# Adapter and MLP with a routed expert: two batches per step, the up projection by seven block products, split weights streamed from DRAM

## The chip, the cores and the metric

One core of one Trainium2 chip runs the whole kernel. The metric is the device time of one execution in microseconds (us), as a median of several executions; 3 runs of the kernel before are known.

## The reference

```python
x = x + L0(x, lang)     # x: 16 batches x 512 tokens x 512
x = x + L1(x, expert)

# L0: adapter with the weights of the batch's language (10 languages)
h = relu(x @ W1[lang] + b1[lang])              # 512 -> 128
u = x + h @ W2[lang] + b2[lang]                # 128 -> 512
L0 = (u - mean(u)) * rsqrt(var(u) + 1e-5) * gamma[lang] + beta[lang]

# L1: MLP; the last 128 output columns come from the batch's expert (8 experts)
h = gelu(x @ W1 + b1)                          # 512 -> 2048, shared weights
L1 = concat(h @ W2 + b2, h @ We[expert] + be[expert])   # 2048 -> 384 | 128
```

All of it is float32.

## The kernel before

Engines are written in raw form: each of PE, ACT, DVE (VectorE), POOL (GpSimd) and SP has its own program, ordered by hand, and waits on semaphores. SP issues all the DMAs. Batches are taken one at a time: the first is unrolled, 14 run in a hardware loop, the last is unrolled (`run`). While the MLP of batch i runs, the adapter of batch i+1 runs in between (`m` in the code).

A float32 operand is split in two rounded halves, hi and lo: ACT copies to a rounded tile (hi), DVE or POOL subtracts (lo), and PE adds three products (`three_passes`, L130 to L132). One such product has a 128x128 stationary and a 128x512 moving operand.

The MLP works on x1T, the transposed input of 4 chunks of 128 features by 512 tokens. For each of the 16 hidden chunks j (HC), `pe_up_step` makes 4 chunks x 3 passes = 12 matmuls into one of two PSUM banks; ACT applies the Gelu (L192) and rounds (L202), DVE makes the lo half (L240). `pe_down_step` for chunk j-2 (LAG) adds 4 token tiles x 3 passes = 12 matmuls to four PSUM banks that stay open over all 16 chunks. At the end DVE adds each bank to the residual tile (L290) and SP stores it.

The split MLP weights w1 and the shared 384 columns of w2 are made once, during the first batch (`load_weights`, `act_weights_hi`, `dve_weights_lo`), and stay in SBUF. The expert's 128 columns are loaded for each batch and split by POOL in 8 pairs of chunks (`pool_expert`, L337 and L339).

Adapter of the next batch: PE up (12 matmuls), PE down (12), 16 transposes of 128x128 (L184); DVE and POOL do the normalization (`dve_moments`, `dve_finish`, `pool_biases` L312 and L314, `pool_rsqrt` L318). POOL also makes the residual tiles (`pool_residual`, L324), which wait until the last store of that tile is done (`out_done`). The numbers XT, A1, RELU, A2 and LN give the hidden chunk beside which each step stands:

```python
XT, A1, RELU, A2, LN = 2, 3, 7, 8, 9
```

## Time and profile before

| | |
|---|---|
| runs, us | 1562.46, 1563.09, 1563.63 (median 1563.09) |
| profiled execution, span from first to last instruction | 1562.4 us |
| PE matmul | 1527.2 us busy (98%), 6784 matmuls |
| DVE | 598.0 us (38%), 948 instructions |
| ACT | 438.6 us (28%), 706 instructions |
| POOL | 620.2 us (40%), 580 instructions |
| DMA | 96.93 MB, mean 62 GB/s |

The profile has no other time for its own execution than the span; it lies 0.7 us under the median of the runs. Busy time counts an instruction from its start to its end. Matmuls overlap, so the step from one start to the next tells what one costs. PEclk in the windows is the granted TensorE clock: 1.00 is 2.4 GHz, 0.50 is 1.2 GHz.

### The profile page before, as it was taken

How to read it: one execution, taken by the hardware profiler on the slowest of the kernel's cores; microseconds unless marked ns; L12 is line 12 of the kernel's file. 1: busy time of each engine (PE TensorE's matmuls, PEld its weight loads, DVE VectorE, ACT ScalarE, POOL GpSimd, SP SyncE). 2: the span in 40 equal slices, each digit the busy share in tenths (PEclk: the TensorE clock that was granted, in tenths of full speed). 3: DMA queues.
4: the chain of work that ended last, by engine and by line, in shares of the span. 5: the costliest groups of instructions: out<-in, count | busy, mean ns of one | idle time of the engine just before them, and what ended most of it. 6: DMA issues, size and time to landing. Idle time of an engine off the chain costs nothing.

```text
span 1562.4 us, 20500 instructions
## 1 busy us (share of the span) xinstructions
PE 1527.2 (98%) x6784; PEld 1255.1 (80%) x6784; DVE 598.0 (38%) x948; ACT 438.6 (28%) x706; POOL 620.2 (40%) x580
## 2 busy tenths in 40 slices
PE   3899999999999999999999999999999999999999
PEld 2678888888888888888888888888888888888887
DVE  6664343432434333344333434334343333443311
ACT  1442222222232322323232222322323223232222
POOL 4464427243262523526244272432625235262300
PEclk7899999999999999999999999999999999999999
DMA  5523013040120402104030130401204021030100
GB/s 177 155 87 114 27 48 92 7 129 10 52 87 10 129 10 87 53 12 124 10 120 20 50 89 7 129 10 57 83 10 129 10 87 52 12 124 10 36 0 27
DMA packets 67121, 96.93 MB, mean 62 GB/s; under 512 B 9632, under 2 KB 30240, under 8 KB 67104
## 3 DMA queue, kind: packets, MB, share of 16 engines
q1 hardware_dynamic: 67104, 96.71, 20.4%
q8 instruction: 10, 0.16, 0.0%
q14 instruction: 7, 0.06, 0.0%
HBM read 79.90 MB, written 16.78 MB: 62 GB/s over the span
## 4 chain that ended last, share of the span: by engine, by line
PE 94%; DMA 2%; DVE 2%; SPq 1%; POOL 1%; issue 0%; ACT 0%; ACTq 0%; POOLq 0%
PE down L130 15%; PE down L132 15%; PE down L131 15%; PE up L132 14%; PE up L130 14%; PE up L131 14%; PE aux L184 2%; PE aux L132 2%; DMA resid<-m_w 2%; PE aux L131 2%; PE aux L130 2%; DVE w_lo L247 1%; DVE x L284 0%; DMA expert_raw<-m_we 0%; SPq L363 0%
## 5 line engine op out<-in xcount | busy, mean ns | idle before, releaser
L240 DVE TENSOR_TENSOR g_lo<-g_raw,g_hi 128x512 fp32r<-128x512 f32 x256 | 224.8, 878 | 696.1 <-ACT g_hi L202 696.0
L130 PE MATMUL down<-w_hi,g_hi 128*128 128x512 f32 x1024 | 407.2, 398 | 0.0
L132 PE MATMUL down<-w_hi,g_lo 128*128 128x512 f32 x1024 | 400.5, 391 | 0.0
L130 PE MATMUL up<-x1T_hi,w_hi 128*128 128x512 f32 x1024 | 399.4, 390 | 0.0
L132 PE MATMUL up<-x1T_hi,w_lo 128*128 128x512 f32 x1024 | 399.1, 390 | 0.0
L131 PE MATMUL up<-x1T_lo,w_hi 128*128 128x512 f32 x1024 | 399.1, 390 | 0.0
L131 PE MATMUL down<-w_lo,g_hi 128*128 128x512 f32 x1024 | 398.6, 389 | 0.0
L192 ACT ACTIVATE g_raw<-up,m_b_sb 128x512 f32<-128x512 f32 x256 | 176.3, 689 | 536.5 <-PE up L132 536.5
L202 ACT CAST g_hi<-g_raw 128x512 fp32r<-128x512 f32 x256 | 159.5, 623 | 485.8 <-PE down L132 483.7
L337 POOL TENSOR_TENSOR w_hi<-expert_raw,ones 128x256 fp32r<-128x256 f32 x128 | 80.7, 630 | 506.0 <-PE down L132 471.1
L132 PEld LDWEIGHTS down<-w_hi,g_lo 128*128 128x128 f32 x1024 | 192.1, 188 | 43.8
L131 PEld LDWEIGHTS down<-w_lo,g_hi 128*128 128x128 f32 x1024 | 192.7, 188 | 40.3
L131 PEld LDWEIGHTS up<-x1T_lo,w_hi 128*128 128x128 f32 x1024 | 192.8, 188 | 40.1
L130 PEld LDWEIGHTS up<-x1T_hi,w_hi 128*128 128x128 f32 x1024 | 192.8, 188 | 40.0
L132 PEld LDWEIGHTS up<-x1T_hi,w_lo 128*128 128x128 f32 x1024 | 192.6, 188 | 40.1
L130 PEld LDWEIGHTS down<-w_hi,g_hi 128*128 128x128 f32 x1024 | 192.3, 188 | 38.6
L318 POOL TENSOR_TENSOR rstd<-var_eps,minus_half 128x1 f32<-128x1 f32 x64 | 63.4, 990 | 317.3 <-DVE var_eps L276 317.3
L339 POOL TENSOR_TENSOR w_lo<-expert_raw,w_hi 128x256 fp32r<-128x256 f32 x128 | 130.9, 1023 | 10.1
L251 DVE TENSOR_TENSOR xT_lo<-xT_raw,xT_hi 128x512 fp32r<-128x512 f32 x64 | 61.2, 957 | 109.4 <-ACT xT_hi L221 109.4
L312 POOL TENSOR_TENSOR x<-x_sb,b_bc 128x512 f32<-128x512 f32 x64 | 94.5, 1476 | 17.3 <-DMA x_sb<-x 15.2
L324 POOL TENSOR_TENSOR resid<-x,m_bias 128x512 f32<-128x512 f32 x64 | 94.6, 1511 | 0.0
L314 POOL TENSOR_TENSOR x_sb<-x_sb,beta_bc 128x512 f32<-128x512 f32 x64 | 84.8, 1325 | 5.0
(44 smaller groups left out, 830.6 us busy)
## 6 DMA issues: line engine op xcount, KB each, us to landing
xT_raw<-xT SPq DMA_DIRECT2D x64, 256.0 KB, 4.1
x_sb<-x SPq DMA_DIRECT2D x64, 256.0 KB, 7.1
expert_raw<-m_we SPq DMA_DIRECT2D x128, 128.0 KB, 2.1
out<-resid SPq DMA_DIRECT2D x64, 256.0 KB, 2.2
a_w_raw<-a_w SPq DMA_DIRECT2D x32, 256.0 KB, 2.8
b_bc<-a_b SPq DMA_DIRECT2D x16, 256.0 KB, 3.7
beta_bc<-a_beta SPq DMA_DIRECT2D x16, 256.0 KB, 5.4
gamma_bc<-a_gamma SPq DMA_DIRECT2D x16, 256.0 KB, 6.8
```

The lines of the kernel that those rows point to most:

```text
L130: eng.matmul(bank, a_hi, b_hi, start=first, stop=False)
L131: eng.matmul(bank, a_hi, b_lo, start=False, stop=False)
L132: return eng.matmul(bank, a_lo, b_hi, start=False, stop=last)
L192: eng.activation(g_raw[:, j % 2, :], up[j % 2][:, :], ACT.Gelu, bias=m_b1_sb[:, j:j + 1]).then_inc(act_g, 1)
L202: eng.copy(g_hi[:, j % 2, :], g_raw[:, j % 2, :]).then_inc(act_ghi, 1)
L240: eng.tensor_tensor(g_lo[:, j % 2, :], g_raw[:, j % 2, :], raw(g_hi[:, j % 2, :]), ALU.subtract).then_inc(dve_glo, 1)
L312: eng.tensor_tensor(x1[:, t, :], x_sb[:, t, :], b2_bc[:, :], ALU.add).then_inc(pool_xb, 1)
L314: eng.tensor_tensor(x_sb[:, t, :], x_sb[:, t, :], beta_bc[:, :], ALU.add).then_inc(pool_xb, 1)
L318: eng.tensor_tensor(rstd[:, t:t + 1], var_eps[:, t:t + 1], minus_half[:, :], ALU.pow).then_inc(pool_rstd, 1)
L324: eng.tensor_tensor(resid[:, t, :], x1[:, t, :], m_bias[:, :], ALU.add).then_inc(pool_res, 1)
L337: eng.tensor_tensor(w2_hi[:, js, cols], expert_raw[:, p % 2, :, :], ones[:, :, :].to_broadcast([P, 2, PART]), ALU.mult).then_inc(pool_eh, 1)
L339: eng.tensor_tensor(w2_lo[:, js, cols], expert_raw[:, p % 2, :, :], raw(w2_hi[:, js, cols]), ALU.subtract).then_inc(pool_e, 1)
```

## The change

Batches are taken in pairs (8 of them: first, 6 in the loop, last), and hidden chunk k is taken with chunk k+8: 8 groups per pair. With A the weights (2 blocks of hidden by 2 blocks of input features) and B the transposed inputs (2 blocks of features by 2 batches), the four outputs C11, C12 (first and second batch, chunk k) and C21, C22 (chunk k+8) are formed from seven products P1 to P7 of sums of blocks. Each product is 2 chunks of 128 features x 3 passes = 6 matmuls.

- A has three given blocks in use as they are, and four sums S1 to S4. POOL makes the sums once, in the first pair, ACT and DVE split all seven (1792 columns a group), PE uses them from one of two slots, and SP writes the split group to DRAM (`keep_w1`, `keep_w2`). In later pairs SP loads group k+1 while k runs: 128x3584 words of w1 and 128x1536 of w2 for each group.
- B has three blocks and four sums T1 to T4, made for each pair from the transposes: DVE sums, ACT rounds, POOL (T) or DVE (B) makes the lo half.
- Three PSUM banks take the products. ACT copies P1 away (s1), DVE makes five sums a group (q, u2, c12, c22, c21), then ACT applies the Gelu.
- The down projection of both batches shares the four banks in turn. A batch keeps them for two groups, then DVE adds them to the residual (`dve_down_sum`).
- The input chunks, adapter and normalization of both batches of the next pair are spread over groups 0 to 7. Both batches of the first pair run their adapter ahead of the first product.

The order in the new kernel, cut to what the prediction speaks of:

```diff
+    def product(eng, bank, k, of_w, of_x, opens, closes):
+        for c in range(2):
+            s = slice(c * P, (c + 1) * P)
+            last = three_passes(eng, bank[:, :], w1[:, k % 2, HI, of_w, s], w1[:, k % 2, LO, of_w, s],
+                                bo[:, of_x, c, HI, :], bo[:, of_x, c, LO, :], opens and c == 0, closes and c == 1)
...
+    def pe_p7(eng, i, k):
+        eng.wait_ge(dve_u2, i.count(GROUPS, k + 1))
+        product(eng, up_b, k, S3, T3, False, False).then_inc(pe_p[7], 1)
...
+    def pe_down(eng, pr, b, k):
...
+        eng.wait_ge(pool_e[b], pr.count(GROUPS, k + 1))
...
     def pe_iteration(eng, i, m):
-        for j in range(HC):
-            pe_up_step(eng, i, j)
...
+        for k in range(GROUPS):
+            pe_p1(eng, i, k)
+            if m and k == 4:
+                pe_adapter_up(eng, m, 1, 0)
+            if m and k == 7:
+                eng.wait_ge(dve_x1, m.count(2 * TT, 2 * TT))
+                pe_transpose(eng, m, 1, 0)
+            pe_p5(eng, i, k)
...
+            if k % 2 == 0:
+                if k >= 2:
+                    pe_down(eng, i, 0, k - 1)
+                elif i is not first:
+                    pe_down(eng, prev, 0, GROUPS - 1)
+            else:
+                if k >= 2:
+                    pe_down(eng, i, 1, k - 2)
+                elif i is not first:
+                    pe_down(eng, prev, 1, GROUPS - 1)
+            if m and k == 1:
+                pe_adapter_up(eng, m, 0, 2)
...
+            pe_p6(eng, i, k)
...
+            pe_p2(eng, i, k)
+            pe_p3(eng, i, k)
...
+            pe_p7(eng, i, k)
...
+            if k % 2 == 0:
+                if k >= 2:
+                    pe_down(eng, i, 1, k - 2)
+                elif i is not first:
+                    pe_down(eng, prev, 1, GROUPS - 2)
+            else:
+                pe_down(eng, i, 0, k - 1)
...
+            pe_p4(eng, i, k)
+            if m and k == 7:
+                eng.wait_ge(dve_blo, m.count(6, 4))
+                eng.wait_ge(dve_t, m.count(8, 6))
+                pe_transpose(eng, m, 0, 2)
...
+    def pool_residual(eng, i, b, t):
...
+        if i is not first:
+            eng.wait_ge(out_done[b][t], i.count(16, 0))
+        eng.tensor_tensor(resid[:, b, t, :], x1[:, b, t, :], m_bias[:, b, :], ALU.add).then_inc(pool_res, 1)
...
+    def pool_iteration(eng, i, m):
...
+            if i is first and k < GROUPS - 1:
+                pool_weight_sums(eng, k + 1)
+            if k == 0:
+                if m:
+                    pool_aw(eng, m, 0, 0)
+                    pool_aw(eng, m, 0, 1)
+                for t in range(TT):
+                    pool_residual(eng, i, 0, t)
+            if k % 2 == 1:
+                pool_expert(eng, i, 0, k - 1)
+                pool_expert(eng, i, 1, k - 1)
+            if k == 1:
+                for t in range(TT):
+                    pool_residual(eng, i, 1, t)
+                if m:
+                    for t in range(TT):
+                        pool_biases(eng, m, 0, t)
...
+            if m and k == 3:
+                pool_aw(eng, m, 1, 0)
+                pool_aw(eng, m, 1, 1)
...
+            if k % 2 == 1:
+                pool_expert(eng, i, 0, k)
+                pool_expert(eng, i, 1, k)
...
     def sp_iteration(eng, i, m, first_expert=None):
...
+        if i is not first:
+            load_w1(eng, i, 1)
+            experts = expert_ids(eng, i)
+        language = languages(eng, m) if m else None
+        for k in range(GROUPS):
...
+            elif 1 <= k < GROUPS - 1:
+                load_w1(eng, i, k + 1)
...
+                if k == 1:
+                    load_xT(eng, m, 0, 2)
+                    load_xT(eng, m, 0, 3)
...
+            if i is not first and k < 2:
+                store(eng, prev, k)
...
+            else:
+                load_w2(eng, i, k)
+            if i is not first or k >= 2:
+                load_experts(eng, k, experts)
```

Two places of the new order. First POOL, in the loop: the residual tiles, the two bias sums of each token tile, and an expert's hi and lo halves. In the kernel before (L300, L302 split the adapter's weights) a batch's residual tiles and biases stand like this:

```order
L302 TENSOR_TENSOR aw_lo<-a_w_raw,aw_hi 128x512
L324 TENSOR_TENSOR resid<-x,m_bias 128x512 x4
L308 ISA
L312 TENSOR_TENSOR x<-x_sb,b_bc 128x512
L313 ISA
L314 TENSOR_TENSOR x_sb<-x_sb,beta_bc 128x512
L329 ISA
L334 ISA
L337 TENSOR_TENSOR w_hi<-expert_raw,ones 128x2x128
L339 TENSOR_TENSOR w_lo<-expert_raw,w_hi 128x2x128
L312 TENSOR_TENSOR x<-x_sb,b_bc 128x512
L313 REGISTER_ALU
```

In the changed kernel, group 1 of a pair in the loop (L781 residual of the second batch, L767 and L769 biases, L788 and L790 hi and lo of the expert for w2; the four bias pairs are alike, and two are left out here):

```order
L781 TENSOR_TENSOR resid<-x_68,m_bias 128x512 x4
L763 ISA
L766 REGISTER_ALU
L767 TENSOR_TENSOR x_68<-xs,vecs 128x512
L768 REGISTER_ALU
L769 TENSOR_TENSOR xs<-xs,vecs 128x512
...
L767 TENSOR_TENSOR x_68<-xs,vecs 128x512
L768 REGISTER_ALU
L769 TENSOR_TENSOR xs<-xs,vecs 128x512
L788 TENSOR_TENSOR w_51<-w_raw,ones 128x2x128
L789 REGISTER_ALU
L790 TENSOR_TENSOR w_51<-w_raw,w_51 128x2x128
```

The expert of group 1 now stands behind all four residual tiles and all eight bias sums; before, an expert stood behind the first two bias sums.

Second DVE, in the loop. In the kernel before, the lo half of an input chunk (L251) stands between two lo halves of the Gelu (L240):

```order
L240 TENSOR_TENSOR g_lo<-g_raw,g_hi 128x512
L250 ISA
L251 TENSOR_TENSOR xT_lo<-xT_raw,xT_hi 128x512
L239 REGISTER_ALU
L240 TENSOR_TENSOR g_lo<-g_raw,g_hi 128x512
```

In the changed kernel, group 1 (L539 is the sum q, L590 an input chunk's lo half, L584 the sum of a down bank, L545 the sum u2):

```order
L539 TENSOR_TENSOR q<-up_c,s_65 128x512
L589 REGISTER_ALU
L590 TENSOR_TENSOR xTs<-xTs_raw,xTs 128x512
L589 REGISTER_ALU
L590 TENSOR_TENSOR xTs<-xTs_raw,xTs 128x512
L583 REGISTER_ALU
L584 TENSOR_TENSOR resid<-down,resid 128x512
L583 REGISTER_ALU
L584 TENSOR_TENSOR resid<-down,resid 128x512
L583 REGISTER_ALU
L584 TENSOR_TENSOR resid<-down,resid 128x512 x2
L545 TENSOR_TENSOR u_66<-up_b,s_65 128x512
```

The down sums and u2 now stand behind the lo halves of two input chunks.

## Rows read from the trace of the kernel before

**Rows 1.** The page: span, busy time, and the chain that ended last
```profile
span 1562.4 us, 20500 instructions
PE 1527.2 (98%) x6784; PEld 1255.1 (80%) x6784; DVE 598.0 (38%) x948; ACT 438.6 (28%) x706; POOL 620.2 (40%) x580
PE 94%; DMA 2%; DVE 2%; SPq 1%; POOL 1%; issue 0%; ACT 0%; ACTq 0%; POOLq 0%
```

**Rows 2.** Window of one batch (length, busy by engine, PEclk, DMA share, GB/s)
```profile
224.48:319.25 94.77, 94.77 (x426) 78.17 (x425) 35.51 (x57) 26.26 (x42) 38.92 (x36) 1.00 0.19 59
```

**Rows 3.** Timeline of PE (start, us): first of 12 down, of 12 up, and next
```profile
201.79 0.40 PE L130 MATMUL down<-w_hi,g_hi 128*128 128x512 f32 x1
...
204.55 0.39 PE L130 MATMUL up<-x1T_hi,w_hi 128*128 128x512 f32 x1
...
207.27 0.39 PE L130 MATMUL aux<-aw_hi,h_hi 128*128 128x512 f32 x1
```

**Rows 4.** Windows of the start (columns as in rows 2)
```profile
10.00:20.00 10.00, 6.45 (x15) 4.19 (x16) 4.42 (x6) 3.11 (x6) 3.15 (x3) 0.87 0.96 304
20.00:30.00 10.00, 4.92 (x10) 2.38 (x9) 9.70 (x15) 1.49 (x4) 9.77 (x8) 0.50 0.77 251
16.00:18.00 2.00, 0.00 (x0) 0.00 (x0) 1.11 (x1) 0.82 (x2) 1.23 (x1) 0.85 1.06 408
```

**Rows 5.** Timeline of DVE: first and last of the four token tiles at the start
```profile
22.97 0.68 DVE L268 TENSOR_TENSOR x<-aux,x 128x512 f32<-128x512 f32 x1
...
35.52 1.76 DVE L284 SCALAR_TENSOR_TENSOR x<-x,rstd,x_sb 128x512 f32<-128x512 f32 x2
```

**Rows 6.** Timeline of PE: idle time and the matmuls around it at the start
```profile
15.09 0.40 PE L132 MATMUL aux<-xT_hi,aw_lo 128*128 128x512 f32 x1
18.73 0.77 PE L130 MATMUL aux<-aw_hi,h_hi 128*128 128x512 f32 x1 [3.25 <-DVE h_lo L256]
37.42 1.94 PE L184 MATMUL aux<-ident,x 128*128 128x128 f32 x8 [9.04 <-DVE x L284]
```

**Rows 7.** Groups of instructions (count, busy us, mean ns, idle before): POOL, DVE, ACT
```profile
L312 POOL TENSOR_TENSOR x<-x_sb,b_bc 128x512 f32<-128x512 f32 x64 | 94.5, 1476 | 17.3 <-DMA x_sb<-x 15.2 <-POOL resid L324 0.2
L314 POOL TENSOR_TENSOR x_sb<-x_sb,beta_bc 128x512 f32<-128x512 f32 x64 | 84.8, 1325 | 5.0
L337 POOL TENSOR_TENSOR w_hi<-expert_raw,ones 128x256 fp32r<-128x256 f32 x128 | 80.7, 630 | 506.0 <-PE down L132 471.1 <-DMA expert_raw<-m_we 34.9
L290 DVE TENSOR_TENSOR resid<-down,resid 128x512 f32<-128x512 f32 x64 | 39.8, 681 | 2.0 <-PE down L132 2.0
L260 DVE TENSOR_TENSOR x1T_lo<-aux,x1T_hi 128x512 fp32r<-128x512 f32 x64 | 42.6, 686 | 76.3 <-ACT x1T_hi L235 76.3
L202 ACT CAST g_hi<-g_raw 128x512 fp32r<-128x512 f32 x256 | 159.5, 623 | 485.8 <-PE down L132 483.7
```

**Rows 8.** Timeline of POOL in the loop: adapter weights' lo half, four residual tiles
```profile
147.87 1.29 POOL L302 TENSOR_TENSOR aw_lo<-a_w_raw,aw_hi 128x512 fp32r<-128x512 f32 x1
151.83 5.95 POOL L324 TENSOR_TENSOR resid<-x,m_bias 128x512 f32<-128x512 f32 x4
```

**Rows 9.** One tile's instructions (ns min/median/max): POOL's residual and expert lo half
```profile
L324 POOL TENSOR_TENSOR resid<-x,m_bias x64: 1287/1295/1747, 94.3 to 1477.3; 128x512 f32<-128x512 f32 x64
L339 POOL TENSOR_TENSOR w_lo<-expert_raw,w_hi x128: 725/1205/1212, 36.8 to 1472.9; 128x256 fp32r<-128x256 f32 x128
```

**Rows 10.** Timeline of SP around the reading of two ids
```profile
129.68 0.33 SPq L381 DMA_DIRECT2D m_bias<-m_be  x1
134.01 0.34 SPq L350 DMA_DIRECT2D a_w_raw<-a_w  x1
```

**Rows 11.** DMA issues (KB each, median us to landing), and landing of xT_raw's
```profile
out<-resid SPq DMA_DIRECT2D x64, 256.0 KB, 2.2
DMA to landing us min/median/max: 2.7/4.1/5.1
```

**Rows 12.** Window of PE's restart at the start (columns as in rows 2)
```profile
43.70:48.20 4.50, 4.50 (x13) 3.54 (x12) 2.83 (x5) 2.45 (x5) 0.00 (x0) 0.51 0.30 98
```

More of the change, by code:

```diff
@@ L75, in build, with sb @@
-    h0_raw = xT_raw[:, 0, :]
-    h0_hi, h0_lo = (sb(f"h0_{h}", [P, TOK], f32r) for h in ("hi", "lo"))
-    b2_bc, gamma_bc, beta_bc = (sb(n, [P, D]) for n in ("b2_bc", "gamma_bc", "beta_bc"))
-    a_b1_sb = sb("a_b1_sb", [P, 1])
+    GROUPS = HC // 2
+    WIDE = PART + SHARED + PART
+    A11, A12, S4, A22, S1, S2, S3 = range(7)
+    B11, B21, B22, T4, T1, T2, T3 = range(7)
+    C11, C12, C22, C21 = range(4)
+    place = [384]
+    def sb(name, shape, dt=f32, over=None):
+        size = 4
+        for n in shape[1:]:
+            size *= n
+        at = place[0] if over is None else homes[over]
+        if over is None:
+            place[0] += (size + 31) // 32 * 32
+        homes[name] = at
+        return nc.alloc_sbuf_tensor_at(name, shape, dt, offset=at)
@@ new lines, in act_xT_hi, with act_relu @@
+    def act_xT_hi(eng, m, b, k):
+        tile, values = xT_tile(m, b, k)
+        eng.wait_ge(in_xT[b][k], m.count(16, 16))
+        eng.copy(tile[:, HI, :], values[:, LO, :]).then_inc(act_xhi, 1)
+    def act_relu(eng, m, b, bank=aux):
+        tile, values = h0_tile(m, b)
+        eng.wait_ge(pe_a1, m.count(2 * KC, (b + 1) * KC))
+        eng.wait_ge(in_b1[b], m.count(16, 16))
+        if m is not first:
+            eng.wait_ge(pe_a2, m.count(2 * TT, b * TT))
+        eng.activation(values[:, LO, :], bank[:, :], ACT.Relu, bias=a_b1_sb[:, b:b + 1]).then_inc(act_h0, 1)
+        eng.wait_ge(act_h0, m.count(2, b + 1))
+        eng.copy(tile[:, HI, :], values[:, LO, :]).then_inc(act_h0hi, 1)
@@ new lines, in store, with languages @@
+    def store(eng, i, b):
+        for t in range(TT):
+            if b == 0:
+                eng.wait_ge(dve_out[0], i.count(4 * GROUPS, 3 * GROUPS + 2 * (t + 1)))
+            else:
+                eng.wait_ge(dve_out[1], i.count(2 * GROUPS, 3 * GROUPS // 2 + t + 1))
+            eng.dma_start(out[i.batch(b), t * P:(t + 1) * P, :], resid[:, b, t, :]).then_inc(out_done[b][t], 16)
+    def languages(eng, m):
+        return [eng.value_load(lang[0:1, bass.ds(m.batch(b), 1)], min_val=0, max_val=LANGS - 1) for b in range(2)]
@@ L591, in _ @@
[L591 to L601 removed]
+            dve_xT_lo(eng, first, 0, 0)
+            dve_xT_lo(eng, first, 0, 1)
@@ L602, in _ @@
+            dve_b_lo(eng, first, B11, 0, up_b)
+            dve_b_lo(eng, first, B11, 1, up_c)
+            dve_t1(eng, first, 0, up_b)
+            dve_t1(eng, first, 1, up_c)
+            dve_t3_t2(eng, first, 0, down[0])
+            dve_b_lo(eng, first, B22, 0, down[0])
+            dve_t3_t2(eng, first, 1, down[1])
+            dve_b_lo(eng, first, B22, 1, down[1])
             run(eng, dve_iteration)
+            dve_sum_c21(eng, last_pair, GROUPS - 1)
+            dve_g_lo(eng, last_pair, GROUPS - 1, C21)
```

1249 lines of the change are left out of this document (819 added, 430 removed).

## The prediction

> **What bounds the kernel now.** I read the page first: PE is 98% busy and 94% of the chain that ended last [rows 1]. Then the windows: one batch of the loop takes 94.77 us, all of them PE, with the clock at its upper level [rows 2]. 16 x 94.77 = 1516.3, so start and tail cost 1562.4 - 1516.3 = 46.1 us. Then PE's timeline for the price of one matmul: 12 down matmuls take 2.76 us, 0.230 each, and 12 up matmuls 2.72 us, 0.2267 each [rows 3]. So a matmul less is time less, as long as nothing else makes PE wait; and everything else stands beside PE with room in it (DVE 38%, POOL 40%). The question is where PE will wait.
>
> **PE's own work.** The seven products of a group are 7 x 6 = 42 matmuls, 336 in a pair instead of 384. 48 x 0.2267 = 10.9 us less in a pair. A pair's work is 189.5 - 10.9 = 178.7 us; eight pairs 1429.3. That is 87 us to win. Without waits a group takes: seven products of 1.36, two down blocks of 24 x 0.23 = 5.5, together 20.6 us; with two adapter pieces of 0.69, 21.9.
>
> **The start, up to the first held down block.** Both batches' adapters now stand ahead of the first product. DVE takes the second batch's second adapter weight ahead of the first token tile, and SP loads it last: behind it in the queue's order are 26 loads of 0.26 MB, 6.8 MB. The start moved 304 and 251 GB/s [rows 4], so 6.8 MB at 278 take 24.5 us, and with the first issues and the ids (some 7 us) it lands at 32. With ACT's and DVE's halves, 0.62 and 0.69 [rows 7], the first token tile starts at 33.5. Before, four tiles took from 22.97 to 35.52 + 1.76 = 37.28, 3.6 us a tile [rows 5]. Eight tiles 28.6, the split of the first 1792 weight columns 2.2 (686 ns for 512 [rows 7], less a fixed part), waits for POOL's reciprocal roots, which now queue behind its biases, 2.4, another half 0.7: 67.4. Then five sets of transposes at the lower clock, 1.94 / 2 = 0.97 each [rows 6], 72.3, P1 75; T1, T3, T2, T4 are made by DVE, ACT and POOL in turn, and POOL's eight lo halves at 1.29 [rows 8] to 1.48 [rows 7] let P6 go at about 81.5 and end at 82.8.
>
> From there POOL has one unbroken list before PE may take the down block of group 1 (it waits for that group's expert, which stands last, as the order shows): weight sums of 256 columns 4 x 0.8 = 3.2 (the size of the lo half [rows 9]), adapter weights 5.1 (lo, hi, lo took 3.96 [rows 8]), four residual tiles 5.95 [rows 8], sums 3.2, two experts 3.6, four residual tiles 5.95, four bias pairs 4 x (1.476 + 1.325 + 0.05) = 11.4, one expert 0.63 + 1.2 = 1.8 [rows 7, 9]: 40.2 us, so the block starts at 123.0. PE's work until then is 14.4 (both adapters, transposes), 11.3 (group 0), 16.4 (group 1) and 3.4: 45.6 at its prices. **Start: 77.4 us lost**, where the kernel before lost 46.1 - 3.4 = 42.7. Bounds: loads at 400 GB/s [rows 4] and POOL's shortest rows give 70; 85 with its longest.
>
> Later in the first pair the weight sums and splits delay POOL's and DVE's lists twice: DVE's 2.3 us ahead of the moments of group 3 and POOL's expert behind them 4.3, group 6 1.0: **5.3** (0 to 10).
>
> **The pairs of the loop.** I follow the waits of one pair; T0, T1 are the starts of its groups 0 and 1.
> - End of group 7: the last B22 chunk is transposed behind the down block; ACT 0.6, then DVE T3, T2 and lo half, 0.65 each [rows 7], before the shared bank is free for the next transpose. It ends 1.3 us after P4, and 0.2 are lost earlier: **1.5**, at 7 boundaries 10.5 (5 to 20).
> - Group 0: SP loads w1 (1.84 MB) when P4 ends (T0 - 1.8) and then reads four ids. Two took 4.0 us [rows 10], so four 8.0; xT is issued at T0 + 6.8 and lands 2.7 later [rows 11], ACT 0.65, twice, DVE's second half ends at T0 + 11.5. Only then DVE adds the down banks, eight pieces 2.9, and makes u2 at T0 + 15.0. P7 could start at T0 + 13.5: **1.5**.
> - Group 1: xT stands behind w2 and experts (issued 1.4 us before T1, 1.05 MB) and w1 (1.84 MB). At 400 GB/s [rows 4] xT lands at T1 + 9.3, its lo half is there at 10.65; the adapter matmul wants it at 8.2: **2.4**.
> - Group 2: DVE's second xT half ends at T1 + 11.4, the first down sum 0.6 later [rows 7], the store 0.4 + 2.2 [rows 11]: T1 + 14.6. POOL's residual tiles wait for it: 5.5 to 5.95, bias pairs 11.3, expert 1.5 to 1.8: 18.6, so T1 + 33.2. PE wants it at T1 + 21.9 + 2.4 + 3.4 = 27.8: **5.4**. Without the late xT it would be T1 + 9.4 + 18.6 = 28.0 against 25.4: 2.6 at least.
> - Group 4: POOL's root of group 3 ends at 19.5, adapter weights 5.1 and expert 1.8 make 26.6; wanted at 26.1: **0.5**.
>
> That is 9.8 us in each of the six pairs of the loop: 58.8 (16 to 90). The last pair has no next one and waits for none of it.
>
> **The clock.** At the start PE had reached its upper level (0.40 for a matmul at 15.09), was idle for 3.25 us, and came back at 0.77 [rows 6]; the granted clock fell from 0.85 to 0.50 around it [rows 4]. A restart ran 4.5 us at 0.51 of the clock [rows 12] and so lost 4.5 x 0.49 = 2.2 us. A wait of 5.4 us is longer than that idle time, so I add 2.2 in each of six pairs and the first: **15.4** (0 to 15.4). The Trainium skill, "TensorE: Matmul & The Clock Gate", section "HAM oscillation — how this bites in real kernels", says the same of kernels whose every tile waits: the array falls back each time and starts cold; by the page's rule the sum stays 1600.1, without it it would be 1584.7. The trace agrees at its start, by the 0.40 and 0.77 above, and has no such gap later.
>
> **Tail:** a down sum 0.68 [rows 7], an issue 0.4 and a store 2.2 [rows 11], as before, and 0.1 for C21's halves: **3.4**.
>
> **Hidden:** w1 and w2 streaming, 3.9 MB in 22 us = 177 GB/s beside 333 to 408 seen; a group's weights have 20 us to land. If they were late, PE would wait at P1 of every group. DVE's five sums, four halves and down sums are 10 us of a group's 20.6; PE would wait at P7 or P4 if they were doubled.
>
> **Sum:** 1429.3 + 77.4 + 5.3 + 10.5 + 58.8 + 15.4 + 3.4 = 1600.1 against the profiled span 1562.4; the median of the runs lies 0.7 above the span, so 1601 against 1563.09: 2.4% slower.
>
> **Rivals.**
> - *The covers hold (faster).* POOL's list in group 1 decides. If xT lands before T1 + 8 and POOL runs at its shortest rows, only the 2.6 of group 2 and the boundary stay, no wait is long enough for the clock, and the start loses 70: 1429.3 + 70 + 3 + 10.5 + 15.6 + 3.4 = 1531.8. It decides where the loop loses under 5 us a pair. For it: DMA is at 62 GB/s now, and large rows may go faster. Against: the list's order is fixed, and its rows are measured. 0.15.
> - *Waits, but the clock stays up.* 1584.7. For it: the waits stand between long busy stretches, which the start doesn't show. 0.20.
> - *POOL and DVE hold each other up.* The residual tile took 1.287 at least and 1.747 at most, the lo half 0.725 and 1.212 [rows 9]. With every row of the list at its longest (7.0 + 14.5 + 1.9 = 23.4, not 18.6) each of seven pairs loses 4.8 more: 1633.7. 0.10. The Trainium skill, "SBUF — State Buffer", section "SBUF: two separate sides", calls the port of DVE and GpSimd an exclusive lock, so that a DVE instruction with two SBUF inputs holds the other off for all of its time; by it the change, which adds such halves on both engines, leans this way. The two lengths in the rows agree with it.
> - *It does not do what it says:* the order shows 42 matmuls in a group; none.
>
> **Chances.** Forecast 0.50, between it and the fast rival around no change 0.05, the rivals 0.15, 0.20, 0.10. A measurement of this kernel can tell about 0.2% from no change (3 us). Faster 0.16, same 0.04, slower 0.80. The range reaches from 1558, which leaves most of the fast rival out, to 1625.
>
> **What would show it.** PE: 6400 matmuls. In the window of a loop pair 190 us or more; PE's waits on POOL's expert lo half about 5 us a pair at group 2, then PEclk below 1.00; on DVE's u2 and xT's lo half 1 to 3 us; SP's waits small. First product at about 72. DVE near 60%, POOL near 50% busy. The forecast is wrong if a loop pair takes under 186 us, or if the first loop pair starts before 250 (178.7 + 77.4 + 5.3 + 1.5 - 14.4 would be 248).

## The result and the profile after

The changed kernel takes 1693.22 us (median of 4 runs, 1691.71 to 1696.68); the kernel before, run beside it, 1562.78 (1562.28 to 1563.63). The ratio is 1.0837, 95% interval [1.0822, 1.0852]: **8.4% slower**. The forecast was 1601 us, slower, with a range of 1558 to 1625: the direction holds, the size doesn't. The profiled execution took 1696.68 us with a span of 1694.9.

The page of the changed kernel (span, busy time, granted clock in 40 slices, DMA by queue, the chain that ended last):

```profile
span 1694.9 us, 20888 instructions
PE 1489.2 (88%) x6400; PEld 1209.6 (71%) x6400; DVE 993.2 (59%) x1620; ACT 521.4 (31%) x822; POOL 722.8 (43%) x672
...
PEclk8579999899999999989999899998999999999999
...
q1 hardware_dynamic: 127664, 264.69, 45.4%
q8 instruction: 64, 1.05, 0.2%
...
PE 54%; issue 17%; POOL 13%; DVE 5%; DMA 5%; ACT 3%; SPq 2%; DVEq 0%; POOLq 0%; ACTq 0%
```

Against [rows 1], PE falls from 94% of the chain to 54%. "Issue" has 17%: time in which an engine waits for nothing that the profile shows. The instruction queue q8 fetched 64 packets where the kernel before fetched 10; its page has

```profile
q8 instruction: 10, 0.16, 0.0%
```

PE's waits over the whole trace (engine, tile and line, what it waited for: us in total, times, longest):

```profile
PE aux L192 <- DVE xTs L590: 49.3, 8, 20.9
PE down L192 <- POOL w L790: 31.4, 12, 5.1
PE up_a L192 <- issue: 30.5, 5, 6.3
PE up_a L192 <- DVE xTs L600: 12.1, 1, 12.1
PE up_a L311 <- DVE x L621: 11.9, 1, 11.9
```

The second row is the wait on GpSimd's expert of the forecast. The third is in no step of it: five times some 6 us. The first is the adapter's matmul on x transposed, with one wait of 20.9 us in the first pair. The last two lie in the start, ahead of the first product. Windows, with the columns of [rows 2], of two loop pairs, of all six, and of the last pair:

```profile
492.76:697.99 205.23, 185.98 (x800) 151.27 (x801) 119.34 (x200) 62.10 (x100) 87.22 (x80) 0.95 0.47 157
697.99:903.00 205.01, 185.28 (x801) 150.68 (x801) 119.11 (x200) 62.18 (x100) 87.54 (x80) 0.96 0.46 158
282.20:1510.80 1228.60, 1114.27 (x4802) 905.91 (x4801) 717.92 (x1201) 372.65 (x600) 523.80 (x481) 0.96 0.46 158
1510.80:1694.90 184.10, 180.61 (x799) 148.87 (x797) 82.56 (x138) 49.43 (x78) 41.71 (x45) 1.00 0.39 138
```

A loop pair takes 205.2 and 205.0 us where I had 192.2; the last pair 184.1 where I had 184.2 (the pair's work without the next batches' adapters, with the held down blocks and the tail). The miss of 1694.9 - 1600.1 = 94.8 us splits into 19.3 up to the first product of pair 1 (282.2, forecast 260.7 + 2.2 for the clock), 75.6 in six loop pairs (1228.6, forecast 1153.0) and -0.1 at the end.

PE's timeline at the loop's back edge, and SP's beside it:

```profile
486.10 0.66 PE L311 MATMUL aux<-ident,x 128*128 128x128 f32 x4 [1.20 <-DVE bo L626]
492.76 0.79 PE L192 MATMUL up_a<-bo,w 128*128 128x512 f32 x1 [6.00 <-issue]
493.35 0.63 PE L193 MATMUL up_a<-bo,w 128*128 128x512 f32 x1
```

```profile
484.93 0.34 SPq L912 DMA_DIRECT2D w<-w_kept  x1
495.46 0.94 SPq L859 DMA_DIRECT2D xTs_raw<-xT  x2
```

The last transposes of a body end at 486.8, product 1 of the next pair starts at 492.8 at half the clock (a matmul each 0.43 us). It happens at five edges, the number of taken branches; not on entering the loop, not on leaving it. In the loop's first pair, where there is no such stop, PE waits 4.5 us on GpSimd's adapter weights in its place:

```profile
299.68 0.79 PE L192 MATMUL aux<-xTs,aw 128*128 128x512 f32 x1 [4.49 <-POOL aw L757]
```

x transposed is issued 10.5 us behind the weights, since SP reads four ids in between (I had 8.0).

In the first pair (PE, then SP):

```profile
119.64 0.79 PE L192 MATMUL aux<-xTs,aw 128*128 128x512 f32 x1 [20.87 <-DVE xTs L590]
```

```profile
67.27 0.42 SPq L907 DMA_DIRECT2D w_kept<-w  x1
103.34 0.64 SPq L923 DMA_DIRECT2D w_kept<-w  x1
...
108.80 0.94 SPq L859 DMA_DIRECT2D xTs_raw<-xT  x2
```

SP stands from 67.7 to 103.3 at the store of the first split down weights (`keep_w2(0)`), which VectorE makes only in group 1; the x-transposed tiles for the adapter's third and fourth piece stand behind it.

**My theory (A)** after this: nothing is wrong with PE's work; the loss is waits that come of the order in the queues of SP and GpSimd, and PE's own code being fetched when its loop branches back, and each such wait lowers the clock for the matmuls behind it. **Rivals:** the 265 MB of DMA, 2.7 times as many as before, are the cause (B); or GpSimd and VectorE are short of time, so that a wait removed comes back elsewhere.

### The profile page after: what moved, and what is told of

The parts are those of the page before. It is cut to its first block, busy times and chain, and to the rows that moved or that the text cites. A ratio compares the mean times of both kernels' runs of the same rounds, so it can differ in the third digit from the quotient of the medians.

```text
span 1694.9 us, 20888 instructions
## 1 busy us (share of the span) xinstructions
PE 1489.2 (88%) x6400; PEld 1209.6 (71%) x6400; DVE 993.2 (59%) x1620; ACT 521.4 (31%) x822; POOL 722.8 (43%) x672
## 4 chain that ended last, share of the span: by engine, by line
PE 54%; issue 17%; POOL 13%; DVE 5%; DMA 5%; ACT 3%; SPq 2%; DVEq 0%; POOLq 0%; ACTq 0%
PE down L192 10%; PE down L194 10%; PE down L193 9%; DMA xTs_raw<-xT 4%; PE up_b L192 3%; PE up_b L194 3%; PE up_b L193 3%; POOL x L767 2%; PE up_a L192 2%; PE up_a L194 2%; PE up_a L193 2%; POOL xs L769 2%; PE up_c L192 2%; PE up_c L193 2%; PE up_c L194 2%
## 5 line engine op out<-in xcount | busy, mean ns | idle before, releaser
L565 DVE TENSOR_TENSOR g<-g_raw,g 128x512 fp32r<-128x512 f32 x256 | 244.7, 966 | 362.6 <-ACT g L419 362.6
L192 PE MATMUL down<-w,g 128*128 128x512 f32 x1024 | 408.4, 399 | 33.3 <-POOL w L790 31.4
L193 PE MATMUL down<-w,g 128*128 128x512 f32 x1024 | 403.8, 394 | 0.0
L194 PE MATMUL down<-w,g 128*128 128x512 f32 x1024 | 403.5, 394 | 0.0
L192 PEld LDWEIGHTS down<-w,g 128*128 128x128 f32 x1024 | 196.0, 191 | 79.1 <-issue 38.2
L788 POOL TENSOR_TENSOR w<-w_raw,ones 128x256 fp32r<-128x256 f32 x128 | 92.8, 725 | 335.0 <-DMA w_raw<-m_we 334.9
L194 PEld LDWEIGHTS down<-w,g 128*128 128x128 f32 x1024 | 195.5, 191 | 42.0
L193 PEld LDWEIGHTS down<-w,g 128*128 128x128 f32 x1024 | 196.2, 192 | 40.2
L419 ACT CAST g<-g_raw 128x512 fp32r<-128x512 f32 x256 | 159.0, 621 | 8.1
L192 PE MATMUL up_b<-bo,w 128*128 128x512 f32 x384 | 154.9, 403 | 4.0 <-POOL bo L798 2.8
L194 PE MATMUL up_b<-bo,w 128*128 128x512 f32 x384 | 153.9, 401 | 0.0
L193 PE MATMUL up_b<-bo,w 128*128 128x512 f32 x384 | 153.8, 401 | 0.0
L192 PE MATMUL up_a<-bo,w 128*128 128x512 f32 x256 | 104.3, 408 | 31.8 <-issue 30.5
L417 ACT ACTIVATE g_raw<-u,m_b_sb 128x512 f32<-128x512 f32 x64 | 46.4, 724 | 274.5 <-PE down L194 240.4
L767 POOL TENSOR_TENSOR x<-xs,vecs 128x512 f32<-128x512 f32 x60 | 90.0, 1501 | 65.1 <-DMA xs<-x 65.1
L781 POOL TENSOR_TENSOR resid<-x,m_bias 128x512 f32<-128x512 f32 x64 | 88.9, 1420 | 59.8 <-DMA out<-resid 59.8
L790 POOL TENSOR_TENSOR w<-w_raw,w 128x256 fp32r<-128x256 f32 x128 | 106.2, 829 | 10.1
L194 PE MATMUL up_a<-bo,w 128*128 128x512 f32 x256 | 102.6, 401 | 0.0
L193 PE MATMUL up_a<-bo,w 128*128 128x512 f32 x256 | 102.6, 401 | 0.0
```

The lines of the kernel that those rows point to most:

```text
L192: eng.matmul(bank, a_hi, b_hi, start=opens, stop=False, skip_group_check=True)
L193: eng.matmul(bank, a_hi, b_lo, start=False, stop=False, skip_group_check=True)
L194: return eng.matmul(bank, a_lo, b_hi, start=False, stop=closes, skip_group_check=True)
L417: eng.activation(values, source, ACT.Gelu, bias=m_b1_sb[:, j:j + 1]).then_inc(act_gelu, 1)
L419: eng.copy(g[:, b, k % 2, h, HI, :], values).then_inc(act_ghi, 1)
L565: eng.tensor_tensor(g[:, b, k % 2, h, LO, :], g_raw[:, b, k % 2, h, LO, :], raw(g[:, b, k % 2, h, HI, :]), ALU.subtract).then_inc(dve_glo, 1)
```

## Experiments: one part at a time

Where one time is given it is one run; the kernel before measured 1561.8 to 1564.2 beside them. The changed kernel's own four runs lie within 5.0 us, so a difference of a few us between single runs says little without its trace.

**1. The loop over pairs written out.**

```diff
-        with eng.Fori(1, PAIRS - 1) as reg:
-            iteration(eng, Pair(reg, 0), Pair(reg, 1))
+        for n in range(1, PAIRS - 1):
+            iteration(eng, Pair(0, n), Pair(0, n + 1))
```

> The changed kernel with its loop over pairs written out: no engine branches back, every instruction and wait otherwise the same. In the changed kernel TensorE stands 6.0 to 6.3 us at each of five back edges of the loop with nothing to wait for that the profile shows, and its first group after that has half the clock for some 3.5 us. Theory A (the 6 us are TensorE's own code being fetched at the branch, because the loop body grew to some 1700 instructions of TensorE): the five gaps go, and with them some of the restarts: 1693 - 5 x 6.1 - up to 5 x 1.9 = 1653 to 1662 us. But product 7's wait on its operand u2 (1.5 us a pair by the prediction), which the gap now covers, may come out: up to 7 us of it back. Theory B (the gap is SyncE's weight load and its traffic, which stretch whatever TensorE then fetches or waits for): the gap moves to another instruction of the same place, a wait of 4 us or more stays at each pair's start, and the time is 1680 to 1695.

1669.96 us. PE around the same place:

```profile
480.36 0.66 PE L311 MATMUL aux<-ident,x 128*128 128x128 f32 x4 [1.20 <-DVE bo L626]
480.77 0.47 PE L192 MATMUL up_a<-bo,w 128*128 128x512 f32 x1
...
496.77 0.77 PE L192 MATMUL aux<-xTs,aw 128*128 128x512 f32 x1 [2.97 <-POOL aw L757]
```

The stop is gone, but 16 us later PE waits 2.4 to 3.0 us a pair on GpSimd's adapter weights, which the stop had covered (they are loaded behind the 1792 KB at the pair's start). So 23 us of the 30.5 are won, less than theory A had.

**2. GpSimd's experts of block 1 ahead of the next batch's biases.**

```diff
+                pool_expert(eng, i, 0, 1)
+                pool_expert(eng, i, 1, 1)
                 if m:
                     for t in range(TT):
                         pool_biases(eng, m, 0, t)
```

(and no longer behind them.)

> The changed kernel with GpSimd's expert weights of down block 1 made before the biases of the next pair's first batch, in place of after them. TensorE now waits 3.3 to 5.1 us a pair for them in group 2, and its first matmuls after that run at the lower clock. Theory A (queue order costs the time): the wait in group 2 goes in all pairs, 7 x 4.4 = 31 us at most, and 7 x 2 of restart: 1648 to 1668 us; if the adapter's wait of group 1 (4 to 4.6 us) stays, nothing of it changes. Theory B (GpSimd and VectorE share a resource and GpSimd is short of time as a whole): the wait moves to the biases or to the sums of group 3 and 4, and the time stays within 5 us of 1693.

1653.37 us: -39.9. The wait in group 2 is gone from every pair and nothing came in its place. Over the four pairs from edge to edge a pair takes 198.0 us in place of 205.0; of the 7.0 won, 1.8 are PE's own busy time (183.5 in place of 185.3: the clock), the rest waits. GpSimd isn't short of time: its list was in the wrong order.

**3. x transposed, tiles 2 and 3, issued in group 0.**

```diff
                 if k == 0:
                     load_x(eng, m, 0)
+                    load_xT(eng, m, 0, 2)
+                    load_xT(eng, m, 0, 3)
```

(and no longer in group 1.)

> The changed kernel with SyncE issuing the next pair's x-transposed loads for groups 2 and 3 in group 0 in place of group 1, so ahead of the weight loads of group 1. Theory A (the wait of 4.05 to 4.57 us in each pair's group 1 is the x-transposed tile standing behind other orders in SyncE's queue): it goes in six pairs, and with it a restart of the clock in each: 6 x (4.3 + up to 2) = 26 to 38 us; the 20.9 us gap of the first pair shrinks too, by 5 to 20 us: 1635 to 1662 us. Theory B (the tile is late because the DMA engines are full of weights then): the loads land later than before after their issue, the wait stays at 3 us or more, 1680 to 1695 us. If the buffers of the transposed tile come free only in group 1, SyncE stands on them and the weights are late instead: over 1693.

1664.29 us: -28.9. The wait on x transposed is gone from the loop pairs (17.4 us in 2 waits, both in pair 0), while the one on the expert grows from 31.4 to 39.4 in all, since PE comes to it sooner. The gain is all in the loop: in the first pair the wait shrinks from 20.9 to 15.1 us, but PE then stands 8.9 us ahead of the first held down block, which starts at 142.4 (140.9 before).

**4. The first pair's store of down weights moved from group 0 to group 1.**

```diff
-                keep_w2(eng, 0)
+            if i is first and k == 1:
+                keep_w2(eng, 0)
```

> The changed kernel with SyncE's store of the first down sums (first pair only) moved from group 0 to group 1, behind the x-transposed loads. SyncE stood 35.6 us on VectorE there, and the x-transposed loads behind it; TensorE had its largest gap, 20.87 us at 119.6, for them. Theory A (that queue order is the gap): the gap shrinks to under 10 us, first down block by 125 to 132 in place of 140.9, in all 8 to 16 us less: 1677 to 1685. Theory B (VectorE's preparation work is the limit in the first pair, whatever SyncE's order): the gap turns up at the next operand, first down block at 138 or later, 1690 to 1694. The loop pairs are the same by both, 205 us.

(This text says down sums; the store is that of the split down weights.) 1683.50 us: -9.7 (its span is 13.2 shorter).

```profile
104.90 0.79 PE L192 MATMUL aux<-xTs,aw 128*128 128x512 f32 x1 [6.85 <-DVE xTs L590]
126.85 0.47 PE L192 MATMUL down<-w,g 128*128 128x512 f32 x1 [2.12 <-issue]
```

The 20.9 us are 6.9, the first held down block starts at 126.9 in place of 140.9. That is near the 123.0 of the forecast, which had everything but this store.

**5. The pair's first weight load behind group 0's other loads.**

```diff
-            load_w1(eng, i, 1)
...
                     load_x(eng, m, 0)
+                    if i is not first:
+                        load_w1(eng, i, 1)
```

> The changed kernel with the weight load at a pair's start (1792 KB, landing in 8 us) issued by SyncE behind group 0's other loads in place of ahead of all. Theory A (TensorE's stop at the back edge is its own code coming in, and no wait on SyncE's work): the stop stays, shorter only by what the load's traffic added to the fetch: 4 to 6.2 us in place of 6.0 to 6.3; the adapter weights and the x-transposed tiles are issued sooner, so that the wait on the x-transposed tile in group 1 shrinks: 1670 to 1690. Theory B (the stop is the traffic of this load): it falls under 2 us in all five places, 1655 to 1670.

1691.06 us, no gain. Four stops of 27.1 us in all and a fifth of 5.92: they grew to 6.6 in the mean, where I had expected 4 to 6.2. Other loads, 1.8 MB of adapter weights, vectors and x transposed, now stand where the weights did. Rival B's form of it (this load and no other) falls too.

**6. The loop written out for TensorE alone.**

> The changed kernel with the pair loop written out for TensorE alone; all other engines branch back as before. With all engines written out the stop at the back edge went (1670.0 us, one run). Theory A (it is TensorE's own branch): the stop is gone here too, 1668 to 1674. Rival (an engine that feeds TensorE stands at its branch, or all stop together): a gap of 3 us or more stays at each pair's first product, 1680 or more.

1678.32 us. All five stops are gone; the adapter weights' wait comes out at 3.3 to 4.0 us. The branch that matters is TensorE's own. So is the instruction queue q8: with TensorE's loop alone written out it falls from 64 packets to 51, what each instruction takes when it is fetched once, and the other instruction queue stays at 45.

```profile
q8 instruction: 51, 0.84, 0.2%
```

The time is 8.4 above that of run 1. Its trace has 22.6 us of the adapter weights' wait against 18.3, and PE is busy for 1489.2 us against 1485.7; why, no run shows.

**7. Streamed loads cut: up weights to a seventh, down weights to a half.**

> The changed kernel with the streamed loads of kept weights cut to a part: a seventh of the up weights (256 in place of 1792 KB) and half of the down weights; the products of later pairs use what stands in the buffers from before, so the result isn't the reference's. DMA bytes fall from 265 MB to about 160 MB. Rival B (streaming, that is DMA bytes, costs the time): the back-edge stop, the wait on the x-transposed tile and the start each shrink; 1600 to 1640. Theory A (queue order and code fetch): the stop at the back edge stays over 4 us; only the x-transposed tile comes sooner by some 3 us, because fewer bytes stand ahead of it: 1660 to 1685.

This kernel leaves out part of the weights' loads, so its output is not the reference's. DMA falls from 266 to 156 MB; 1650.55 us, -42.7, between the two theories. The row of the second edge, and two windows in the stop:

```profile
478.82 0.79 PE L192 MATMUL up_a<-bo,w 128*128 128x512 f32 x1 [3.65 <-issue]
474.97:476.80 1.83, 0.20 (x2) 0.00 (x0) 0.99 (x2) 0.77 (x2) 0.29 (x1) 1.00 0.44 146
476.80:478.60 1.80, 0.00 (x0) 0.00 (x0) 1.47 (x3) 1.16 (x2) 1.26 (x1) 0.74 0.00 0
```

The stop shrinks from 6.1 us to 3.4 to 3.7, under the 4 that theory A had, and the wait on x transposed is gone in the loop. So the streams do cost time, though PE never waited on them: they make other transfers late, the code among them. More than half of a stop stays without them. In the second half of this one no transfer starts (share 0.00), so a part of the stop isn't transfer.

## Experiments: all parts together

**8. All five edits at once.**

> The changed kernel with all five edits: loop written out, expert weights of block 1 ahead of the biases, x-transposed tiles 2 and 3 issued in group 0, the first pair's store of down sums behind them, the pair's first weight load behind group 0's others. Singly (each against 1693.2) they gave -23.2, -39.8, -28.9 and -9.7. Theory A (all of the loss beyond the start is queue order and code fetch, and the parts don't touch each other): -102 and the adapter weights' wait that the first edit bared (2.4 to 3 us a pair) gone too: 1573 to 1591. If the covers hold fully (no gap over 1.5 us after the first pair): about 1550 to 1573. Rival (the waits give way to one another, since GpSimd and SyncE have too little time as a whole): 1600 to 1630.

1570.68 us: -122.5, more than the sum of the four that gained (101.8). The waits that single edits bared or lengthened are gone too: no wait on adapter weights is left (18.3 us in run 1), and the expert's 8.0 more of run 3 don't appear. PE now waits on the weight load of edit 5 (10.1 us in 6 waits), and comes back at the lower clock behind three of them, of 2.2 to 3.2 us.

**9. That load behind the adapter's vectors.**

> The kernel with all five edits (1570.7 us), its pair's first weight load issued behind the adapter's vectors in place of behind all loads of group 0. There group 1's first product waited 2.2 to 3.2 us a pair on this load and then ran at the lower clock. Theory A: that wait goes and the adapter weights still come in time: 6 x (2.4 + up to 1.9) = 14 to 26 us less, 1545 to 1557 us. Rival (the load now delays x or the x-transposed tiles, 2 MB behind it): another wait of 2 us or more in groups 0 to 2, 1562 to 1575.

1554.46 us: -16.2, that wait is gone.

**10. The start in another order as well:** on PE, ScalarE and VectorE the first batch's down products, ReLU and moments ahead of the second batch's adapter up, and SP loads the first batch's second adapter weights ahead of its vectors. PE's part:

```diff
-            for k in range(KC):
-                pe_adapter_up(eng, first, 1, k, up_a)
             for b in range(2):
+                if b == 1:
+                    for k in range(KC):
+                        pe_adapter_up(eng, first, 1, k, up_a)
                 for t in range(TT):
                     pe_adapter_down(eng, first, b, t, down[t])
```

> The kernel before in this list with its start in another order: the first batch's adapter down products, ReLU and moments ahead of the second batch's adapter up, and the down weights of its adapter loaded ahead of its vectors. VectorE worked through eight token tiles from 33.3 us to 66.7, 3.7 us for each, after waiting for both batches' weights. Theory (VectorE's eight tiles in a row set the start, and they began late for an order only): they begin by 20 to 24 us, the first product of seven at 58 to 63 in place of 70: 8 to 12 us less than that kernel, 1535 to 1549 us, faster than the kernel before by 1% or more. Rival (the start is bound by loads, GpSimd's sums or the weights' preparation after the first products): 0 to 4 us less.

1548.68 us (4 runs, 1547.94 to 1549.17), ratio 0.9902 to the kernel before, interval [0.9886, 0.9919]: **1.0% faster than the kernel before**. The start gave 5.8 us, between theory and rival: PE now waits 12.3 us at 36.6 for the second batch's weights, whose split stands behind VectorE's moments. Two of its loop pairs (columns as in [rows 2]):

```profile
444.28:627.98 183.70, 179.09 (x803) 146.92 (x802) 118.27 (x201) 61.80 (x100) 88.51 (x81) 1.00 0.52 175
627.98:811.69 183.71, 179.12 (x803) 146.93 (x802) 118.88 (x201) 61.83 (x100) 87.80 (x81) 1.00 0.51 176
```

PE is busy for 179.1 us, the forecast's 178.7, and the clock never falls. In the changed kernel the same matmuls took 186.0 and 185.3 in the two windows above: **6.2 to 6.9 us of a pair were the lower clock**.

**11. The same with the loop kept.**

> The same as the kernel before in this list, with the loop over pairs kept. Theory A (TensorE's fetch at the back edge is a cost of its own, of 6 us and a slower restart at five edges): 5 x (6 to 8) = 30 to 40 us more than with the loop written out. Rival (it was partly SyncE's weight load at the same moment, which is now issued later): 15 to 30 us more, each gap 3.5 to 5 us.

1601.60 us, 52.9 more: both theories were too low. PE's row at the second edge, and windows up to it:

```profile
453.80 0.79 PE L192 MATMUL up_a<-bo,w 128*128 128x512 f32 x1 [9.26 <-issue]
```

```profile
446.00:448.00 2.00, 0.00 (x0) 0.00 (x0) 1.66 (x3) 0.82 (x2) 0.30 (x1) 0.50 0.84 117
448.00:450.00 2.00, 0.00 (x0) 0.00 (x0) 1.20 (x2) 0.52 (x1) 0.97 (x1) 0.50 0.95 202
450.00:452.00 2.00, 0.00 (x0) 0.00 (x0) 0.00 (x0) 0.00 (x0) 0.00 (x0) 0.50 1.06 431
```

Five stops of 41.0 us in all and five restarts at 2.3 make 52.5 of the 52.9. The DMA engines are nearly full throughout the stop (share 0.84 to 1.06): some 3.6 MB of loads were issued just ahead of the branch. Four stops take 8.4 to 9.3 us; the fifth, where the share falls to 0.52 for 2 us, takes 5.5. With little, some and much of such traffic (runs 7, the changed kernel, 11) a stop is 3.5, 6.1 and 8.2 us in the mean, 9.3 at most.

## Experiments: why the edge stops

**12. The kernel before, its loop written out** (the control), and **13. the kernel before with two batches to a body:**

```diff
-        with eng.Fori(1, BATCHES - 1) as reg:
-            iteration(eng, Batch(reg, 0), Batch(reg, 1))
+        with eng.Fori(1, BATCHES // 2) as reg:
+            iteration(eng, Batch(Twice(reg), -1), Batch(Twice(reg), 0))
+            iteration(eng, Batch(Twice(reg), 0), Batch(Twice(reg), 1))
```

> The control: the kernel before with its loop over batches written out. Its loop body has 424 matmuls in place of 800, and its trace shows no stop at the back edge. Theory A: no change, within 0.2% of 1562.8. If branches cost something there too that the trace hides: 2 to 14 us less.

> The kernel before with two batches to a turn of its loop: TensorE's body has 848 matmuls in place of 424, as many as the changed kernel's (800), and the rest, loads among it, is that of the kernel before. Written out whole it measured no change (0.9999). Theory A (the back-edge stop comes with the length of TensorE's body): a stop of 3 us or more appears at the loop's back edges (six), 6 x (3.5 to 9) = 20 to 55 us more, 1583 to 1618. Rival (it comes with something else of the changed kernel: its streamed loads, its place between products): no stop, within 0.3% of the kernel before.

Run 12: ratio 0.9999, interval [0.9989, 1.0008]. Run 13: 1.0014, [1.0005, 1.0024]. My theory that the stop comes with a long body fell: TensorE's body has 848 matmuls, the instruction queue fetches it anew on every turn (68 packets, against 55 with the loop written out in run 12 and 10 in the kernel before), and the worst it shows is 0.33 us.

```profile
q8 instruction: 68, 1.11, 0.3%
```

```profile
712.58 0.49 PE L142 MATMUL up<-x1T_hi,w_hi 128*128 128x512 f32 x1 [0.33 <-issue]
```

What differs is what stands ahead of the branch. TensorE's instructions at the end of the changed kernel's body, and then of run 13's, in the order they were written, with what each waits for:

```
L194 MATMUL up_b<-bo,w_49 128x512
L391 REGISTER_ALU
L311 MATMUL aux<-ident,x_68 128x128 [waits dve_t,dve_blo]
L311 MATMUL aux<-ident,x_68 128x128 x3
L1016 REGISTER_ALU
L1016 COMPARE_AND_BRANCH
```

```
L142 MATMUL down<-w_hi,g_hi 128x512 [waits dve_glo]
L143 MATMUL down<-w_lo,g_hi 128x512
L144 MATMUL down<-w_hi,g_lo 128x512
...
L144 MATMUL down<-w_hi,g_lo 128x512
L544 REGISTER_ALU
L544 COMPARE_AND_BRANCH
```

The changed kernel reaches its branch with 0.7 us of work still queued behind the last wait, run 13 with 12 matmuls (8 of them stand at the "..."), 2.7 us.

**14. The branch moved, nothing else:** the last piece of the body (a set of transposes, product 4 of group 7, the last transposes) becomes the first of the next turn, so that 12 matmuls of down block 6 stand between the last wait and the branch.

```diff
+        if i is not first:
+            eng.wait_ge(dve_blo, i.count(6, 3))
+            eng.wait_ge(dve_t, i.count(8, 4))
+            pe_transpose(eng, i, 1, 3)
+            pe_p4(eng, prev, GROUPS - 1)
+            eng.wait_ge(dve_blo, i.count(6, 4))
+            eng.wait_ge(dve_t, i.count(8, 6))
+            pe_transpose(eng, i, 0, 2)
         for k in range(GROUPS):
```

> The changed kernel with the back edge of TensorE's loop moved back by six matmuls and two sets of transposes: the branch now stands behind down block 6's 24 matmuls, 12 of which follow their last wait (2.7 us of queued work), in place of behind four transposes that follow a wait (0.7 us). Order of work, waits and loads are the same otherwise. Two batches to a body in the kernel before had no stop, though TensorE's body is as long and its code was fetched anew on each turn; its branch stands behind 12 matmuls too. Theory A (TensorE's sequencer reaches the branch only after the last wait, and the fetch is hidden by what is queued then; with SyncE's 1792 KB load issued only after product 4, its traffic comes behind the fetch too): the stop of 6.0 to 6.3 us falls to 0 to 2 us, five times 4 to 6, but the waits on x-transposed tiles and adapter weights behind it come out as in the kernel with the loop written out (1670.0): 1668 to 1680. Rival (the body is fetched from the start only after the branch is taken, whatever is queued): the stop stays at 4 us or more, 1685 to 1695.

**15. The same in the kernel of run 11.**

> All edits with the loop kept (1601.6 us), and the back edge moved in the same way. There the stop was 8.6 to 9.3 us, with 1.8 MB of adapter loads and 1.8 MB of weights in the queues at the branch. With the loop written out the same kernel took 1548.7. Theory A: the stop falls to 0 to 4 us (the adapter loads, issued before product 4, still stand ahead of the fetch): 1550 to 1575. Rival: 1590 to 1602.

Run 14: 1682.13 us, 11.1 less; no stop is left at any edge, and as in runs 1 and 6 the adapter weights' wait (3.5 to 3.9 us) comes out, which takes more of the gain than I allowed (2 us beyond theory A's range). Run 15: 1553.07 us (4 runs), 48.5 less than run 11, ratio 0.9939 to the kernel before, interval [0.9922, 0.9955]. It is 0.6% faster than the kernel before, with the loop kept. Its second edge, and its instruction queue:

```profile
444.81 0.65 PE L311 MATMUL aux<-ident,x 128*128 128x128 f32 x4 [1.29 <-DVE bo L627]
445.22 0.47 PE L192 MATMUL up_a<-bo,w 128*128 128x512 f32 x1
```

```profile
q8 instruction: 64, 1.05, 0.3%
```

The same 64 packets are fetched as in the changed kernel; only PE no longer stands still for them. So what the stop comes from is shown: TensorE fetches its body anew at each taken branch, the stop is longer the more DMA is under way, and none is seen where matmuls are queued behind the last wait.

The trace's records of the instruction queue show it packet by packet. In all 15 stops of the changed kernel and runs 7 and 11 PE resumes 1.7 to 1.9 us behind the end of one 16 KB packet of q8, which takes 0.9 to 1.0 us. The stops differ by when that packet starts. At the second edge it is 1.6 us behind the start of the last transposes in run 7 (476.1), 3.9 us in the changed kernel (490.0) and 7.2 us in run 11 (451.1), as more loads stand ahead of it. In run 14 the packet comes at 476.8, under down block 6, and ends 2.1 us before the first instruction of the new turn starts (479.82).

The moved branch changes two things at once, the work queued at it and the traffic around it. Windows around it in run 14 and in run 15 (both second edges):

```profile
474.00:478.00 4.00, 4.00 (x21) 3.33 (x20) 2.74 (x6) 3.80 (x7) 3.08 (x5) 1.00 0.02 6
478.00:482.00 4.00, 3.82 (x19) 2.83 (x17) 4.00 (x4) 1.11 (x3) 4.00 (x3) 1.00 0.01 4
```

```profile
436.00:440.00 4.00, 4.00 (x19) 3.25 (x19) 2.74 (x5) 3.75 (x7) 3.84 (x5) 1.00 0.01 4
```

The DMA engines are all but idle there (share 0.01 to 0.02), as in run 13 (0.00 and 0.03 in the 4 us ahead of its edge), while the changed kernel has 0.97 and 0.96 in the middle of its stop. Quiet alone doesn't remove a stop: run 7 still had 3.4 to 3.7 us. So of run 11's 8.2 us a turn some 3.5 go to the queued work and the rest to the quieter stretch, an estimate from runs 7 and 11; no run has queued work with full DMA engines.

## Why the prediction was right and wrong, by its steps

- **PE's own work: right.** 178.7 us a pair; 179.1 measured with the clock up. The 87 us were there to win.
- **The start up to the first product: right.** 72 forecast, 70.7 measured; product 6 at 81.5 against 81.2.
- **The start up to the first held down block: failed.** "From there POOL has one unbroken list" took GpSimd for the only engine behind, and had 123.0; it was 140.9. I never followed SP's list through the first pair, where it stands 35.6 us at one store. Run 4 shows it: 126.9 without. Most of the first pair's 19.3 us are this (13.2 less span in run 4).
- **Later in the first pair** (5.3 for two delays): five smaller gaps of 1.3 to 2.3 us. Not tested.
- **End of group 7: undersized.** 1.5 a pair; measured 1.47, 0.95 and 1.20, 3.6 in three waits. I had seen the last one only.
- **The sign on the first loop pair: summed wrong.** "Before 250" had 248 for its start. The first pair has both own adapters (+14.4) and leaves three down blocks to the next (-16.6), so the same terms give 260.7, not 248; 282.2 was measured.
- **Group 0:** the 1.5 us on u2 didn't show in any pair. GpSimd's adapter weights come first there, which had no step: 4.5 us in the loop's first pair, and 2.4 to 3.0 in run 1. In the other pairs the stop at the edge covered them. The ids took longer than my 8.0 us: x transposed left 10.5 us behind the weights.
- **Group 1: mis-sized.** 2.4 forecast, 4.05 to 4.57 measured. I let x transposed land in the time of its bytes, at T1 + 9.3; in the second loop pair ACT gets it at 528.4, which is T1 + 11.5. Its median landing time is 6.9 us against 4.1 before [rows 11].
- **Group 2: right.** 5.4 forecast, 3.3 to 5.1 measured; run 2 shows the mechanism. **Group 4:** 0.5 forecast, 0.9 measured.
- **The clock: price right, count wrong.** "I add 2.2 in each of six pairs" counted one restart a pair, behind the wait of group 2. There were three: behind the edge (in the loop's first pair behind the adapter weights), behind group 1's wait and behind group 2's. PE was busy 1114.3 us in six pairs and would be 6 x 179.1 = 1074.6: 39.7, or 18 times 2.2. By the rival in which the clock stays up it would be none. The Trainium skill, "TensorE: Matmul & The Clock Gate", section "HAM oscillation — how this bites in real kernels", says that an array which waits in every tile starts each anew from the cold level; the trace agrees in every pair, by a granted clock of 0.50 behind all 18 of these waits (3.3 to 6.3 us). At 14 of them the first matmul already takes 0.77 to 0.80 us. Behind group 1's wait in the last four loop pairs it takes 0.50, and the clock falls 1 us later, as here behind the one that ends at 734.60:

```profile
734.60:735.50 0.90, 0.90 (x4) 0.77 (x5) 0.90 (x2) 0.00 (x0) 0.00 (x0) 1.00 0.00 0
735.60:738.90 3.30, 3.30 (x9) 2.55 (x8) 2.64 (x5) 0.00 (x0) 0.35 (x1) 0.50 0.57 208
```

- **What had no step: the stop at the back edge,** 30.5 us and, through the clock, 11 more. I had looked for new waits on other engines' work, never on PE's own code. The row was there to see: the page's instruction queue, 10 packets before. The Trainium skill, "Runtime: NRT & Kernel Launch", section "Instruction fetch mechanics", says that a taken branch to code the engine no longer holds must wait for a DMA fetch. The trace agrees for this kernel (five taken branches, five stops of 6.0 to 6.3 us).
- **Hidden streaming: half right.** PE never waited on a streamed weight in the changed kernel, but run 7 shows 42.7 us that its bytes cost through others.
- **The rival in which POOL and DVE hold each other up (0.10): not the cause.** It had GpSimd's list of group 2 at 23.4 us in place of 18.6 and the wait 4.8 longer. In the second loop pair the list, residual tiles to expert, runs from 533.65 to 553.04, 19.4 us, and no wait of group 2 was over 5.1 us. Single rows do vary (a residual tile 1.27 to 3.07 us); what of that is the shared port, no run here shows.

The 75.6 us that six loop pairs took beyond the forecast: stops 30.5, clock 39.7 - 13.2 = 26.5, matmuls 6 x 0.4 = 2.6, and 16.0 in the other waits (114.3 of idle time less 30.5, against 67.8). Of those 16.0, the ends of group 7 make 12.7 and group 1 11.7, group 4 2.3; groups 0 and 2 came out 4.5 and 6.3 shorter than forecast.

## What to carry to other kernels

When a change doubles a loop body, walk every queue engine's list through the first turn and through one steady turn, and ask of each order what stands behind it: three of the waits here were a matter of order, and once the order was mended the same products beat the kernel before by 1%. Look at what stands between the last wait and TensorE's branch: work that is queued there hides the fetch of the next turn's code, and moving the branch in front of the last waits, and with it the fetch ahead of the pair's loads, gave 48.5 us in run 15. Price each wait of more than 2 us on TensorE with the restart of its clock behind it (2.2 us here), and count all of them; a wait that is removed can bare or lengthen the next one, so edits together can give more than the sum of each.

## What was not expected of the hardware

- A body of code is fetched anew on each turn without a trace in the time, where 2.7 us of work is queued at the branch and the DMA engines are quiet (run 13: 68 packets, +0.14%), and costs 3.4 to 9.3 us a turn with 0.7 us queued.
- The stop grows with the DMA that is under way: 3.5 us in run 7 (share 0.44, then 0.00), 9.3 us in run 11 (0.84 and more).
- Waits as short as 2.2 us brought the clock to its lower level (run 8, 0.80 for the first matmul). The same wait of 2.30 us in the first pair did so in the changed kernel, 1 us behind its end, and not in run 10 (granted clock 1.00 from 160 to 172 us). So the first matmul behind a wait doesn't tell whether the clock falls.
